# Splitting the second thought's odd weight pairs between the two thoughts

## The reference, cut to what matters

```python
def ffn(x):                                   # used twice, same weights
    thought = layer_norm(x)[:, -1, :] @ agg_w + agg_b        # last token of each sequence
    for _ in range(4):
        t = gelu(layer_norm(thought) @ d1_w + d1_b)          # (2, 4096)
        thought = thought + (t @ d2_w + d2_b)                # (2, 1024)
    gate = sigmoid(x @ gate_w + gate_b)                      # every token
    return layer_norm(x + gate * (thought @ bc_w + bc_b)[:, None, :])
x = x + 0.5 * ffn(layer_norm(x))
x = x + attention(layer_norm(x))    # windows of 128, weights relu(q k / 128)^2, then w_o
x = x + 0.5 * ffn(layer_norm(x))
```

## Time and profile of the kernel before

| | us |
|---|---|
| median of 3 runs | 2104.93 |
| the profiled execution | 2105.51 |
| its span, first to last instruction | 2104.3 |
| PE busy | 2012.6 (96%) |
| DVE busy | 1208.7 (57%) |
| ACT busy | 682.8 (32%) |
| granted TensorE clock, mean | 0.986 |
| moved by DMA | 555.78 MB, mean 264 GB/s |

### The profile page before, as it was taken

One profiled execution on the slowest core, in us unless ns is written; L12 is line 12 of the kernel. 1 busy time (PEld: TensorE's weight loads), 2 busy tenths in 40 slices (PEclk: granted clock), 3 DMA queues, 4 the chain that ended last, 5 costly groups with the idle time before them and its releaser, 6 DMA issues. The chain is left out here.

```text
span 2104.3 us, 30594 instructions
## 1 busy us (share of the span) xinstructions
PE 2012.6 (96%) x12010; PEld 1026.0 (49%) x12010; DVE 1208.7 (57%) x2152; ACT 682.8 (32%) x947; POOL 162.0 (8%) x278
## 2 busy tenths in 40 slices
PE   8998879999999999998999999999999999999997
PEld 3333333344333447655565556665556564444443
DVE  2322665334433466666766655655565535888887
ACT  0577444233223232223333212121212113444443
POOL 0000010000000010010000000000000001111111
PEclk9999989999999999999999999999999999999999
DMA  8689686999999843358989798898987947555552
GB/s 341 239 324 408 238 290 251 345 327 353 362 346 355 347 161 101 101 163 314 323 291 345 262 319 295 290 356 291 312 292 282 328 172 199 153 154 154 151 150 80
DMA packets 275214, 555.78 MB, mean 264 GB/s; under 512 B 149040, under 2 KB 149248, under 8 KB 274688
## 3 DMA queue, kind: packets, MB, share of 16 engines
q1 hardware_dynamic: 275072, 553.83, 76.2%
HBM read 406.93 MB, written 113.26 MB: 247 GB/s over the span
## 5 line engine op out<-in xcount | busy, mean ns | idle before, releaser
L1062 PE MATMUL product_banks<-gate_arena,arena 128*128 128x512 f16 x1536 | 359.8, 386 | 0.0
L1062 PE MATMUL product_banks<-wide_a,thought_units 128*128 128x512 f16 x1536 | 331.7, 379 | 1.0 <-DVE arena L1697 1.0
L1062 PE MATMUL product_banks<-gate_arena,wide_a 128*128 128x256 f16 x2688 | 308.8, 275 | 2.5 <-DMA gate_arena<-arena 2.5
L1062 PE MATMUL product_banks<-wide_b,gate_arena 128*128 128x512 f16 x1344 | 301.8, 379 | 0.0
L1062 PEld LDWEIGHTS product_banks<-gate_arena,wide_a 128*128 128x128 f16 x2688 | 261.0, 99 | 60.1 <-issue 28.9
L1062 PEld LDWEIGHTS product_banks<-gate_arena,arena 128*128 128x128 f16 x1536 | 146.8, 100 | 207.3 <-issue 57.9
L1062 PEld LDWEIGHTS product_banks<-wide_a,thought_units 128*128 128x128 f16 x1536 | 150.2, 98 | 182.8 <-DVE arena L1697 1.8
L1062 PEld LDWEIGHTS product_banks<-wide_b,gate_arena 128*128 128x128 f16 x1344 | 127.2, 98 | 167.5 <-issue 24.9
L1486 DVE BATCH_NORM_STATS2 bn_parts<-arena 128x6 f32<-128x512 f32 x256 | 164.2, 683 | 4.4
L1909 POOL TENSOR_TENSOR token_stats<-stats,minus_half 128x1 f32<-128x1 f32 x96 | 62.8, 654 | 1115.0 <-DVE stats L1494 938.4
L1511 DVE SCALAR_TENSOR_TENSOR arena<-product_banks,inverse_gate,arena 128x512 f32<-128x512 f32 x64 | 47.8, 748 | 174.4 <-PE product_banks L1062 174.2
(11 more groups left out here) (206 smaller groups left out, 2280.0 us busy)
## 6 DMA issues: line engine op xcount, KB each, us to landing
thought_units<-parts_scratch SPq DMA_DIRECT2D x268, 512.0 KB, 6.3
thought_units<-in_d_w SPq DMA_DIRECT2D x148, 512.0 KB, 7.3
thought_row<-in_d_w SPq DMA_DIRECT2D x76, 512.0 KB, 6.8
arena<-in_x SPq DMA_DIRECT2D x64, 512.0 KB, 8.6
parts_scratch<-thought_units SPq DMA_DIRECT2D x64, 512.0 KB, 5.8
x_scratch<-arena SPq DMA_DIRECT2D x64, 512.0 KB, 7.2
arena<-x_scratch SPq DMA_DIRECT2D x40, 512.0 KB, 6.5
gate_scratch<-arena SPq DMA_DIRECT2D x32, 512.0 KB, 7.8
```

What stands on the lines that cost most here:

```text
L1062: mm = pe.matmul(bank, left(i, k), right(j, k), start=(n == 0), stop=(n == 3 * KD - 1))
```

## The change

Two kinds of work move, and nothing is added to or taken from PE.

- **Splits.** All pairs of the second thought are now of the form *pair*, in step 0 too. The 16 odd pairs (32 units) are split and stored by a new list, `THOUGHTS.between`, which `paced` spreads at 0.8 pieces per PE piece over the gates of tiles 28 to 31 and groups 0 and 1. Its fetches use slots 0 and 1, its parts slots 2 and 3. In step 0 of the second thought those stored parts are fetched back, 32 fetches that were not there. Slots 4 to 7 are free to that thought's fetches from its beginning.
- **`gate_save`.** The eight stores move from the stretch of tiles 9 to 27, where they were mixed into the list of splits of the folded weights (0.65 pieces per PE piece), to behind the gates of tiles 28 to 31, two behind each. The list that they have left is shorter and goes at 0.5 per PE piece; `params` goes in at its eighth place.

```diff
@@ class Thoughts
-        for tau in range(2):
-            self.think(tau)
+        self.think(0)
+        self.split_rest()
+        self.think(1)
...
     def use_of(self, owner):
         kind, n = owner
+        if kind == "tokens" or kind == "split" and self.splits[n].unit is None:
+            return "again"
...
-        if (tau, step) == (0, 1):
+        if slots is not None:
+            pass
+        elif (tau, step) == (0, 1):
             slots = FOR_FIRST if how == "keep" else FOR_LOADS
         else:
-            slots = FOR_LOADS + (FOR_FIRST if tau == 0 else FOR_SPLITS if step else [])
+            slots = FOR_LOADS + (FOR_SPLITS if tau else FOR_FIRST)
...
-        return "keep" if step == 0 and pair % 2 else "pair"
+        return "pair"
+
+    def split_rest(self):
+        pairs = [("d1", [(k, c), (k, c + 1)]) for c in range(0, COLS_1, 2) for k in range(1, KD, 2)]
+        pairs += [("d2", [(k, 0), (k + 1, 0)]) for k in range(2, KH, 4)]
+        self.between = []
+        for matrix, pair in pairs:
+            made = []
+            for k, c in pair:
+                at = len(self.splits)
+                load = self.load(None, None, matrix, k, c, "keep", at, FOR_LOADS[:2])
+                slot = FOR_LOADS[2 + at % 2]
+                self.splits.append(Split(load, None, slot, self.take(slot, ("split", at))))
+                made.append(at)
+            for kind in ("high", "low"):
+                for at in made:
+                    self.between.append(self.step(None, (kind, at)))
+
+        for slot in FOR_SPLITS:
+            self.take(slot, ("tokens", (slot - FOR_SPLITS[0]) // GROUP))
@@ whole_plan
-    save = [("params",)] + [("rest",)] * 5 + [("half_params",)]
-    for k in range(KD):
-        save += [("gate_save", k)] + [("rest",)] * 3
-    splits = paced(splits, save, 0.75)
+    splits[8:8] = [("params",)] + [("rest",)] * 5 + [("half_params",)]
     splits += [("prep_fetch", 0), ("rest",), ("rest",), ("prep_norm", 0), ("prep_beta", 0)]
-    gates = paced([p for n in range(EARLY, TILES - LATE) for p in plan_gate(n)], splits, 0.65, PE_PIECES)
+    gates = paced([p for n in range(EARLY, TILES - LATE) for p in plan_gate(n)], splits, 0.5, PE_PIECES)
...
-    out += paced([p for n in range(TILES - LATE, TILES) for p in plan_gate(n)], prep, 1.15, PE_PIECES)
-    out += [("sigmoid", TILES - 1, 1), ("gate_store", TILES - 1)]
-    out.append(("score_scale",))
-    out += plan_stage_2(0, B)
+    late = []
+    for n in range(LATE):
+        late += plan_gate(TILES - LATE + n) + [("gate_save", k) for k in range(2 * n, 2 * n + 2)]
+    between = paced(late, prep, 1.15, PE_PIECES)
+    between += [("sigmoid", TILES - 1, 1), ("gate_store", TILES - 1)]
+    between.append(("score_scale",))
+    between += plan_stage_2(0, B)
+    out += paced(between, THOUGHTS.between, 0.8, PE_PIECES)
     out += with_thought(plan_stage_2(B, GROUPS - 1), THOUGHTS.beats[1])
@@ await_left
-        if kind == "split":
-            eng.wait_ge(unit_used, SPLITS[n].unit + 1)
+        if kind == "tokens":
+            eng.wait_ge(product_full, BANK_AT[("v", n, GROUP - 1, HALVES - 1)] + 1)
+        elif kind == "split":
+            if SPLITS[n].unit is not None:
+                eng.wait_ge(unit_used, SPLITS[n].unit + 1)
             await_stored(eng, n)
@@ t_high on ACT
-                if n == STORE_2 or n == STORE_2 + GROUP:
-                    act.wait_ge(product_full, BANK_AT[("score", (n - STORE_2) // GROUP, 0)] + 1)
```

More of the change, by code:

```diff
@@ L118 @@
     load: int
-    unit: int
+    unit: int | None
     slot: int
@@ L158, in take, with load @@
         return before
-    def load(self, tau, step, matrix, k, c, how, used):
+    def load(self, tau, step, matrix, k, c, how, used, slots=None):
         n = len(self.loads)
-        if (tau, step) == (0, 1):
+        if slots is not None:
+            pass
+        elif (tau, step) == (0, 1):
             slots = FOR_FIRST if how == "keep" else FOR_LOADS
         else:
-            slots = FOR_LOADS + (FOR_FIRST if tau == 0 else FOR_SPLITS if step else [])
+            slots = FOR_LOADS + (FOR_SPLITS if tau else FOR_FIRST)
         slot = min(slots, key=lambda at: self.taken_at.get(at, -1))
@@ L282, in put, with step @@
         made = []
-        for kind, *info in beat:
-            step = Think("t_" + kind, (tau, *info), [], *self.counts)
-            self.counts = [a + b for a, b in zip(self.counts, RAISES[kind])]
-            made.append(("t_" + kind, step))
-            if kind in ("whole", "whole_top"):
-                self.by_use["whole", step.whole] = step
-            elif kind in ("unit", "pair"):
-                self.by_use["unit", step.unit] = step
-            elif kind == "low":
-                self.by_use["low", info[0]] = step
-            elif kind == "scales":
-                self.by_use["scales"] = step
-        self.beats[tau].append(made)
+        for piece in beat:
+            made.append(self.step(tau, piece))
+        self.beats[tau].append(made)
+    def step(self, tau, piece):
+        kind, *info = piece
+        step = Think("t_" + kind, (tau, *info), [], *self.counts)
+        self.counts = [a + b for a, b in zip(self.counts, RAISES[kind])]
+        if kind in ("whole", "whole_top"):
+            self.by_use["whole", step.whole] = step
+        elif kind in ("unit", "pair"):
+            self.by_use["unit", step.unit] = step
+        elif kind == "low":
+            self.by_use["low", info[0]] = step
+        elif kind == "scales":
+            self.by_use["scales"] = step
+        elif kind == "rows" and tau == 1:
+            self.by_use["again"] = step
+        return ("t_" + kind, step)
 THOUGHTS = Thoughts()
@@ L818, in await_left @@
             eng.wait_ge(unit_low, LOADS[n].used + 1)
-    last_split = {}
-    for n, split in enumerate(SPLITS):
-        last_split[n * 2 // len(SPLITS), split.slot] = ("split", n)
+    last_split = {split.slot: ("split", n) for n, split in enumerate(SPLITS) if split.slot in FOR_SPLITS}
     def await_thoughts(eng):
```

3 lines of the change are left out of this document (1 added, 2 removed).

## The result

The changed kernel takes 2145.66 us (median of four runs, 2139.86 to 2147.12) against 2104.05 us for the kernel before: a ratio of 1.0185, with a 95% interval of 1.0171 to 1.0199. It is 41.6 us slower, where 2099 us was forecast, and outside the range of 2080 to 2122 us. The profiled execution has a span of 2143.7 us, 39.4 us over that of before.

The account below looks back on a forecast made before the run. PE was taken as the bound, busy 2012.6 of 2104.3 us, so only its 92 us idle and its clock could move. -18 - 8 + 20 = -6 from 2105.5 us profiled gave 2099.5, written 2099; range 2080 to 2122.

Parts of the forecast that it names:

- Rival 2: Between the thoughts, ACT's wait and fetch behind store become the bound, 11.3 us a pair: 2119 us, chance 0.26.
- Step C: Splits moved between the thoughts, over gates 28 to 31 and groups 0 and 1: +20 us, bounds 0 and +43.
- Their engine time hides: Between the thoughts, the splits' added 37 us on ACT and 41 us on DVE were taken to cost nothing.
- 10.3 us each: Turn of one pair's chain, from five intervals ending the first thought's splits; between the thoughts it would need 154 us.
- I give it 5 us: Between the thoughts, PE can run ahead of ACT by part of a gate or its banks: 5 us allowed.
- so +3: Clock lost between the thoughts as PE idles in lumps, some of them short: +3 us.
- +17: Loss taken for the stretch between the thoughts, between the chain's +20 and the queues' +15 to +18, before the clock.
- Moved waits: ACT's first query write waits for stores behind tile 31's gate: cost 0, a few us if SP is over 10 late.
- The second view: Queues between the thoughts: 160 us of queue time, at least +15; by bytes no loss to +18.
- Step A: Second thought's step 0 without its splits loses PE's late-fetch gaps and low clock: -18 us, bounds 0 and -22.
- Step B: Gates' weight stores leave tiles 9 to 27, shortening PE's waits on fetches there: -8 us, bounds 0 and -14.
- What would show it: Signs listed for each step, such as waits, clock, DMA share and 160 to 167 us from tile 28 to group 2.

Follow-up runs that it names:

- e10_tiny_hl: Changed kernel with highs and lows between the thoughts working on only 64 of 1024 columns, transfers whole: 2123.3 us.
- the kernel with A alone: Changed kernel without any split between the thoughts, the second thought fetching even pairs' parts instead of the odd ones': 2091.6 us, ratio 0.9919.

## Why the prediction was wrong

**The rival that came true** is the second, slower by the chain between the thoughts, though its 2119 us was far too mild and its mechanism, one chain of ACT's wait and fetch, is a part only. It put the loss at the right place, with its point of decision: at 10.5 us a pair the change breaks even, and the pair took 12.1.

**Step C, forecast +20 and at most +43, measured +54.4.** This is the step that failed, in four of its terms.

1. *"Their engine time hides: ACT gains 37 us on 43 and DVE 41 us on 91 of 145."* It was a mean over a stretch. The runs with tiny highs and lows gave 22 us back. The trace of before could have told: DVE's idle time there was lumped (9.5 us in one wait for group 1's inputs, 13.8 us in six waits for ACT between a query's high and low parts, in the rows below), and the waits of PE at collects on DVE and ACT say that these engines come last at the end of each group. A pair's 2.6 us on DVE was to be counted in full, sixteen times: 41 us as an upper bound. (Rival 2 has DVE busy 0.60 there; it was 90.6 of 145 us, 0.62.)
2. *"10.3 us each"*, the turn taken from the end of the first thought. The fetches landed sooner here than there (5.1 against 6.5 us), yet the turn was 12.1: in rows 7 DVE was busy 18.7 of 57 us, between the thoughts 0.64 of the time, and each turn also carries the other work of both queues. The prediction saw this ("against a DVE that was nearly free in rows 8") and left it to the rival.
3. *"I give it 5 us"* for PE running ahead, and one sum for the whole stretch. The lateness is not made up in group 0 but handed on: group 1's inputs stand in SP's list behind the last lows of the gates, and were issued 19.6 us behind the gates' end. Eighteen us of group 0 go with this. It is not SP's list alone, as they were 15.9 us late without the splits in it. That list was read for the first query's wait alone; "Moved waits" names group 1's fetches as what stands behind the stores, and doesn't ask who waits for them.
4. *"so +3"* for the clock. The term started from the 288 us stretch (5.8 us lost on 16.5 us idle) and was lowered for short gaps. Measured are 12.6 us, as the gaps came in six lumps of 3.9 to 12.3 us; the old ratio on 41.8 us of idle time would have given 14.7. That idle time is the larger part of the miss: +41.8 us where +17 had been taken.

DVE's waits in the kernel before from 732 to 877 us, for the first term:

```profile
DVE gate_arena L1666 <- ACT gate_arena L1393: 13.8, 6, 3.2
DVE arena L1620 <- DMA arena<-gate_scratch: 9.5, 1, 9.5
```

The second view, the queues (+15 to +18), was the wrong bound to lean on. Its sum of 160 us of queue time was right: the queues were busy 0.79 of 199.9 us, which is 158 us, and 0.90 of 177.7 us in e10_tiny_hl, which is 160. But this is a bound from below, and the stretch took 40 us more; by the runs the transfers cost 29 us mostly through their waits, not through full queues. The rate by the Trainium skill's limit in "DMA: Bandwidth & Descriptors" (Specifications, 358 GB/s) wasn't tested either way: the stretch moved 270 GB/s.

**Step A, forecast -18, measured -12.4** (the kernel without step C is 13 us faster in all). The mechanism held, the size not: PE's idle time in the 288 us fell from 16.5 to 2.6 us and the clock went to 1.00, as written. The term that was missing is the later steps: there PE is idle 6.4 us of 527 where it was 2.2 of 535, and the clock is 0.99. The waits that came are on the small chain of the thought itself (3.7 us on DVE for a turn of its sums in the kernel with A alone), at other places than before. Over the whole second thought PE's idle time fell by 9.7 us and its busy time by 2.7. The prediction also read the waits at the collects there as a late ACT or DVE; rows 3 put them down to issue, which names no one.

**Step B, forecast -8, measured 0.** The weakest step: PE's waits on the thought's fetches in tiles 9 to 27 were 14.2 us and are 14.5 us now. The share of the queues fell only from 0.92 to 0.90, and the fetches were as late as before: they are late for another reason, the lower bound that the text named and didn't take. Which reason was not tried.

**What would show it.** The signs named were right ones: no wait over 2 us on stored parts and a clock of 1.00 in step A; waits under 8 us for step B (they were 14.5, and say that B failed); over 175 us of stretch for the second rival (199.9). A DMA share of 0.85 to 0.95 was expected and 0.79 came, with the queue time as summed: the stretch was longer than its queues needed.

What stays open: why eight of the sixteen splits in the second thought, set one pair in four, or ten of them, the last ten odd pairs, made that thought 15 to 18 us longer than all sixteen at one pair in two; and how the 54 us divide exactly, as the single savings (29 for the transfers, 22 for the operations) were measured each with the other in place, and no kernel had both small.

## What to carry to other kernels

An idle share is not room: before work is moved beside other work, look at who PE waited for last in that stretch, and if it was the engine that gets the work, count every us of it in full as the upper bound. An engine that stands in its queue for a transfer hands the wait to all behind it and to the engines that wait for those, and the lateness is carried over the next stage's first fetches, which stand in the same lists. The largest wait in the table (here ACT's 78 us for fetches) is not the one to remove: follow PE's own waits back, and look at what came last there. Here the relieved stretch had 16.5 us of idle PE and some clock to give, 13 us in all by the run without the splits; the work moved was 77 us of two engines' time and 64 transfers: bound the gain first, and ask of such a cost what would hide it.

## What the runs showed of the hardware that I had not expected

A fetch of 512 KB behind a store landed 4.3 to 6.8 us after its issue (5.1 in the median) with the queues busy 0.8, no longer than the fetches of the kernel before with the queues busy 0.4 (5.7 us in the median). Of 32 KB, with 32 KB stores ahead, it still took 1.8 us. The same DMAs from POOL's queue made each pair 0.8 us longer (12.9 against 12.1 us) though POOL had been busy only 0.10 of the stretch. And the clock's part is not small: over the 200 us between the thoughts it was granted 0.87 in the mean, on 45 us of waits. Each of the six waits, 3.9 to 12.3 us long, was followed by 3 to 6 us of work mostly at the lower of its two levels, 1.2 GHz, and these cost 12 us more.
